# A decoder block on one Trainium2 core: chained VectorE work dealt out in single steps, rows reloaded a stage earlier, the turns' order changed

## What is computed

```
x = x + attn(layernorm(x), Wq, bq, Wk, bk, Wv, bv, Wo, bo)        # 16 heads of 128
x = x + xattn(layernorm(x), ctx, ctx, gamma)                     # 8 heads of 64 channels, over channels
x = x + ffn(layernorm(x), ternary(w1), ternary(w3), ternary(w2))  # hidden 1365, silu gate
```

## Time and profile before

| | us |
|---|---|
| median of 3 runs (1170.23 to 1171.52) | 1171.01 |
| the profiled execution | 1170.35 |
| its span, first to last instruction | 1168.6 |
| PE busy | 1118.9 |
| DVE busy | 743.5 |
| ACT busy | 551.6 |
| POOL busy | 461.0 |

### The profile page before, as it was taken

One profiled execution on the slowest core, in us unless ns is written; L12 is line 12 of the kernel. 1 busy time (PEld: TensorE's weight loads), 2 busy tenths in 40 slices (PEclk: granted clock), 3 DMA queues, 4 the chain that ended last, 5 costly groups with the idle time before them and its releaser, 6 DMA issues.

```text
span 1168.6 us, 15784 instructions
## 1 busy us (share of the span) xinstructions
PE 1118.9 (96%) x5792; PEld 938.8 (80%) x5792; DVE 743.5 (64%) x1389; ACT 551.6 (47%) x1145; POOL 461.0 (39%) x400
## 2 busy tenths in 40 slices
PE   4999999989999999999999999989999999999997
PEld 4888888868888788888888888768878887887776
DVE  7555547887757677765423325878767876787431
ACT  2455673324242366577514223267628753774230
POOL 1322327331432265664334030157517642764030
PEclk9999999999999999999999999999999999999999
DMA  7466654434433634312521022271113111310000
GB/s 234 132 181 180 197 162 138 163 112 146 143 115 121 204 91 120 98 37 98 225 72 55 18 97 82 94 201 47 46 56 107 46 47 64 99 46 11 27 1 36
DMA packets 53846, 121.13 MB, mean 104 GB/s; under 512 B 10009, under 2 KB 10009, under 8 KB 51722
## 3 DMA queue, kind: packets, MB, share of 16 engines
q1 hardware_dynamic: 53770, 120.13, 32.6%
HBM read 102.27 MB, written 17.84 MB: 103 GB/s over the span
## 4 chain that ended last, share of the span: by engine, by line
PE 83%; DVE 7%; ACT 4%; issue 2%; POOL 2%; DMA 1%; SPq 0%; POOLq 0%; DVEq 0%; ACTq 0%
PE bank L150 17%; PE bank L151 17%; PE bank L152 17%; PE bank L538 6%; PE bank L539 6%; PE bank L501 4%; PE bank L552 4%; PE bank L553 4%; PE bank L523 2%; PE bank L524 2%; PE bank L511 2%; PE bank L512 2%; POOL wal L1917 1%; DMA kd<-in_ctx 1%; ACT wah L1378 1%
## 5 line engine op out<-in xcount | busy, mean ns | idle before, releaser
L538 PE MATMUL bank<-x3h,w 128*128 128x512 f32 (+1 forms) x352 | 141.8, 403 | 2.4 <-DVE x3l L795 1.7
L1356 ACT ACTIVATE yh<-bank 128x512 fp32r<-128x512 f32 x64 | 38.1, 600 | 214.2 <-PE bank L152 214.1
L539 PE MATMUL bank<-x3l,w 128*128 128x512 f32 (+1 forms) x352 | 138.9, 394 | 0.0
L875 POOL TENSOR_SCALAR pe_x<-pe_x,xri,gam 128x512 f32<-128x512 f32 x96 | 75.6, 788 | 79.7 <-DVE xri L726 75.6
L150 PE MATMUL bank<-yh,rh 128*128 128x512 f32 x256 | 101.1, 395 | 6.0 <-DVE xacc L1779 6.0
L150 PE MATMUL bank<-wah,gh 128*128 128x512 f32 x256 | 103.9, 406 | 2.6 <-POOL wal L1917 1.3
L1917 POOL TENSOR_TENSOR wal<-raw_a,wah 128x512 fp32r<-128x512 f32 x44 | 59.7, 1382 | 117.2 <-ACT wah L1378 117.2
L722 DVE TENSOR_REDUCE xmx<-bank 128x1 f32<-128x512 f32 x128 | 87.5, 683 | 24.1 <-PE bank L512 23.3
L1922 POOL TENSOR_TENSOR wbl<-raw_b,wbh 128x512 fp32r<-128x512 f32 x64 | 88.6, 1408 | 36.0 <-ACT wbh L1398 35.8
L1615 DVE TENSOR_TENSOR yl<-bank,yh 128x512 fp32r<-128x512 f32 x64 | 44.0, 690 | 90.8 <-ACT yh L1356 90.6
L150 PE MATMUL bank<-wah,ph 128*128 128x512 f32 x256 | 100.4, 392 | 0.3 <-POOL wal L1917 0.3
(11 more groups left out here) (171 smaller groups left out, 3026.5 us busy)
## 6 DMA issues: line engine op xcount, KB each, us to landing
raw_a<-in_wk SPq DMA_DIRECT2D x8, 1024.0 KB, 5.3
raw_b<-in_wq SPq DMA_DIRECT2D x8, 1024.0 KB, 5.3
raw_a<-in_wo SPq DMA_DIRECT2D x8, 1024.0 KB, 5.1
raw_b<-in_wvt SPq DMA_DIRECT2D x8, 1024.0 KB, 4.9
ternary_scratch<-wraw SPq DMA_DIRECT2D x24, 341.2 KB, 2.9
x1d<-x_scratch SPq DMA_DIRECT2D x48, 128.0 KB, 3.1
kd<-in_ctx SPq DMA_DIRECT2D x48, 128.0 KB, 3.1
w<-ternary_scratch SPq DMA_DIRECT2D x2, 2730.0 KB, 10.8
```

What stands on the lines that cost most here:

```text
L538: pe.matmul(u_bank[w][0:m, :], lhs, x3h[:, c, :], start=c == 0, stop=False)
L539: mm = pe.matmul(u_bank[w][0:m, :], lhs, x3l[:, c, :], start=False, stop=c == CK - 1)
L875: pool.tensor_scalar(m.pe_x[:, q, :], m.pe_x[:, q, :], xri[:, q:q + 1], gam[:], ALU.mult, ALU.mult).then_inc(s["xpn"], 1)
```

## The change

- **Linked chains.** `newton_rsqrt` becomes `newton_step(k)`, one step a call. `bst`, `mvar`, `rstd`, `ntmp` and `nvar` get a place for each of two sequences. Four `bn_aggr` now share one link, and so do two `bn_stats`. In pass 0 (`dve_next_rows`) both sequences' moments come first, then their Newton steps together (128x8 elements) in two slots of six and seven steps, then the eight row tiles. `dve_x1` of sequence 1 goes one step (of `X1_STEPS` = 15) per early step 1 to 15; those of sequences 2 and 3 one step per step 1 to 30 of turn 1.
- **Rows of sequence 0.** They are loaded into a buffer of their own (`x2back`) in group j = 1 of pass 1; their moments, Newton steps and normalisation (`dve_back`) lie behind the `yl` splits of groups 1, 2 and 3. The rows to keep are loaded by a DMA (`sp_x2_kept`) and no longer copied, and the 1 MB load of sequence 1's x2 is issued before the last `out` tiles, ahead of the 2.7 MB load of w2, where it came behind it.
- **Turns.** `pe_vt` goes to the end of its step, behind the `pe_up` piece, for heads 0 and 4 one step later (`values_step`: steps 1, 8, 17, 24); `dve_vt` and `act_vt` move with it. The first `pe_up` piece of turns 2, 3 and last is made in two halves of 256 columns, each waiting for its own two `x3l` tiles. `pe_down` waits for each chunk's `gtl` by itself; tile 0 is split 5 and 6 chunks around a `pe_pt`, tile 1 3 and 8 around a `pe_ret`. The kept rows of turns 2, 3 and last are copied by POOL (`pool_keep`) instead of ACT.
- On SP the store of sequence 1's statistics goes behind group 3's loads, that of sequence 2 behind head 6.

```diff
@@ dve, linked chains
-    for _ in range(3):
+def newton_step(dve, link, y, tmp, v, k):
...
+        def dve_moments_in(dve, link, p, i, half):
+            dve.wait_ge(s[("xn_a", "xn_b")[half] + str(i)], 16 * (p + 1))
+            for j in (2 * half, 2 * half + 1):
+                ins = dve.bn_stats(bst[:, i, j, :], xnf[i][:, j, :])
+            link(ins)
+        def dve_aggregate(dve, link, i):
+            for j in range(TJ):
+                ins = dve.bn_aggr(mvar[:, i, j, :], bst[:, i, j, :])
+            link(ins)
...
+        def dve_next_rows(dve, link, part):
+            if 0 <= part < 4:
+                dve_moments_in(dve, link, 1, part // 2, part % 2)
+            elif part in (4, 5):
+                dve_aggregate(dve, link, part - 4)
+            elif part == 7:
+                for k in range(0, RSTD_STEPS // 2):
+                    dve_rstd(dve, link, slice(0, PB), k)
+            elif part == 8:
+                for k in range(RSTD_STEPS // 2, RSTD_STEPS):
+                    dve_rstd(dve, link, slice(0, PB), k)
+            elif 9 <= part < 9 + PB * TJ:
+                dve_normalise(dve, link, (part - 9) // TJ, (part - 9) % TJ)
...
-        def dve_early_values(dve, n):
+        def dve_early_values(dve, link, n):
             h, q = divmod(n, 4)
+            if 0 <= n - 1 < X1_STEPS:
+                dve_x1(dve, link, PASSES - 2, 1, n - 1)
...
             def attention_rest(n):
-                if n in (6, 10):
-                    dve_x1(dve, link, PASSES - 1, 1, n == 10)
+                i, k = divmod(n - 1, X1_STEPS)
+                if 0 <= i < PB:
+                    dve_x1(dve, link, PASSES - 1, i, k)
@@ rows of sequence 0
+        x2back = put("x2back", 112 * KB, [P, TJ, C])
...
         def sp_x2_back(sp):
-            sp.wait_ge(s["a_ready"], A["Y", PASSES - 1, GROUPS - 1, 0, CK - 1] + 1)
-            sp.dma_start(main.x2[:], x1_dram[0].rearrange("(t p) c -> p t c", p=P)).then_inc(s["x2_back"], 16)
+            sp.wait_ge(s["ptl"], GROUPS * (PASSES - 1) + 2)
+            sp.dma_start(x2back[:], x1_dram[0].rearrange("(t p) c -> p t c", p=P)).then_inc(s["x2_back"], 16)
...
                     dve_between(dve, link, p, j, c)
-                    if last and not further and c + 1 < CK:
-                        dve_moments_back(dve, c)
+                    if j and not further:
+                        dve_back(dve, link, CK * (j - 1) + c)
@@ stage_b_sp
-            sp_x2_back(sp)
...
             sp_head(sp, main, 1, 0)
             sp_head(sp, main, 1, 1)
+            sp.dma_start(main.x2[:], x1_dram[1].rearrange("(t p) c -> p t c", p=P)).then_inc(s["x2_in"], 16)
+            sp_x2_kept(sp)
             sp_x1_data(sp, p, 0)
-            sp_x1_stat(sp, p, 0)
             sp_x1_data(sp, p, 1)
             sp_head(sp, main, 1, 2)
             sp_w2(sp)
-            sp.wait_ge(s["x2_kept"], TJ)
-            sp.dma_start(main.x2[:], x1_dram[1].rearrange("(t p) c -> p t c", p=P)).then_inc(s["x2_in"], 16)
@@ turns
+        def values_step(h):
+            return 4 * h + (h % 4 == 0)
...
+            for cols in (slice(0, T // 2), slice(T // 2, T)) if piece == 0 and f else (slice(0, T),):
+                if piece == 0:
+                    pe.wait_ge(s["t_free"], t_x3(f, cols.stop // P))
...
-        def pe_down(pe, f, t):
-            pe.wait_ge(s["gl2"], 1 + f * HC + HC)
+        def pe_down(pe, f, t, chunks=range(HC)):
...
+                if t == 0:
+                    pe.wait_ge(s["gl2"], 1 + f * HC + i + 1)
...
-                        if q == 0 and h % 2 == 0:
-                            pe_vt(pe, main, b, h)
...
+                    if b is not None and h % 2 == 0 and values_step(h) == 4 * h + q:
+                        pe_vt(pe, main, b, h)
...
+                pe_down(pe, f, 0, range(0, HC // 2))
...
+                pe_down(pe, f, 0, range(HC // 2, HC))
...
+                pe_down(pe, f, 1, range(0, 3))
...
+        def pool_keep(pool, f, t):
+            pool.wait_ge(s["x3n"], (f + 1) * TJ)
+            pool.wait_ge(s["y_out"], 1 + f * (16 * TJ))
+            pool.tensor_copy(x2res[:, t, :], x2[:, t, :]).then_inc(s["x2_kept"], 1)
```

More of the change, by code:

```diff
@@ L892, in pool_turn @@
                 if f is not None:
+                    if f and n < TJ:
+                        pool_keep(pool, f, n)
                     for piece in pieces(n - GATE_LAG):
@@ L1889, in _ @@
             link = make_link(dve, "link", chain)
-            for part in range(LN_PARTS):
-                dve_normalise(dve, link, 0, 0, part)
+            dve_rows(dve, link, 0, 0)
             for j in range(TJ):
```

203 lines of the change are left out of this document (107 added, 96 removed).

## The result

The changed kernel takes **1157.24 us** (median of four runs, 1156.49 to 1157.44); the kernel before took 1170.62 on the same chip. The ratio is 0.9885, with a 95% interval of 0.9868 to 0.9902. The profiled execution took 1157.29, its span is 1155.5. The gain is 13 us; 20.7 were forecast.

A forecast was written before the change was run, and what follows sets the result against it. The prediction took TensorE (PE) to bound the kernel, busy 1118.9 us of 1168.6. Its terms summed to 20.7 us less than the profiled 1170.35, so 1149.65, with the median forecast at 1150; range 1144 to 1158.

The forecast's parts named there:

- rival 1: VectorE becomes the bound in turn 1, with small steps of 0.55 us filling its free time; 7.5 more, 1157 us; 18%.
- Start (-0.6): Before PE's first matmul: fewer links among `bn_aggr` and `bn_stats` bring DVE's first rows earlier, 0.6 us gained.
- Pass 0 (-5.1): Pass 0: without the late chain, PE's 4.02 us wait and the half clock go, 0.8 lost again; 5.1 us gained.
- Early steps (-0.4): Early steps of pass 1: a wait goes with the `dve_x1` lump (-1.4), fifteen single steps cost +1.0; 0.4 us gained.
- End of pass 1 (-1.9): End of pass 1: two PE waits of 0.8 us behind chains go, the moved chain costs 0; 1.9 us gained.
- Turn 1 (-1.1): Turn 1: step 10's lump goes (-2.8), `kd` lands earlier (-1.5), single steps cost +2.5, the start +0.7; 1.1 us gained.
- Values in mid-turn (-1.5): Middle of each turn: three waits of 0.6 us for `vts` go (-2.3), `dve_ret` costs +0.25 each; 1.5 us gained.
- Ends of turns (-5.1): Ends of turns 1 to 3: `pe_down` matmuls cover waits of 0.96 and 0.47 us; 1.7 gained each, 5.1 in all.
- Starts of turns 2 and 3 (+0.6): Starts of turns 2 and 3: no gain from the moves, `pool_keep` makes the first `pe_pt` late; +0.3 us each.
- Last turn (-0.9 and -4.7): Last turn: half the first piece precedes the last `x3l` (-0.9); `pe_down` needn't await all `gtl`, no half clock (-4.7 us).
- "Turn 1 about 87 us": Sign for turn 1: first score tile to last `pe_up` takes about 87 us instead of 90.1.
- Rival 3: Turn 1 and early steps: each small non-aggregating step waits for a whole POOL operation; 13 us slower, 1184; 3%.

The follow-up runs named there:

- six and six steps: Changed kernel with the twelve Newton steps of sequence 0's rows six and six behind the second and third `yl` of group 2, not four, four, four; 1156.58 us.
- faster version: Changed kernel with values at old place in turn 1, at new place with `dve_q` first in turns 2 and 3, Newton steps six and six; 1144.95 us.

## Why the prediction was right, and where it was not

Direction and range were right; 1157.2 is 7 us above the forecast time. It is the very number of rival 1, and rival 1 was wrong: its sign was a mean small step over 0.6 us in turn 1. The 38 small chain instructions there take 9.0 us in all, 0.24 each, which is also under the 0.4 forecast.

That the time stayed in the range is in part luck. With the values at their old place the turns take 4.7, 0.2 and 0.2 us less than before, where the forecast without the values' terms had 1.8 less in turn 1 and 0.3 more in each of the others. The move itself added 4.6, 2.1 and 2.3, where its terms come to +0.2, -0.5 and -0.5. So the move was forecast wrong by nearly 10 us, the rest of the turns made good some 4, and the range had been drawn wide for rivals that did not happen.

- *Start (-0.6).* Right by the first matmul, which shared links bring 0.56 us earlier in the mean of the executions. In the table it doesn't show, since the clock rose to full at 18.4 us in the one execution and at 19.8 in the other.
- *Pass 0 (-5.1).* Right: -5.1. The rounding instructions are still blocked (1.64 and 2.00 us at 236 and 238), and the bank still comes in time, all but 0.29. The cause was only half seen: with one link for the `bn_aggr` the lump costs 1.6, not 5, so most of this gain could have come from the links alone.
- *Early steps (-0.4).* -0.7; not tested alone.
- *End of pass 1 (-1.9).* Both waits went. The step that failed is "with POOL's splits later in the group: 0". The fourth `yl` is where POOL's splits of the next load begin; four Newton steps met them, 1.7 us of PE. The row to ask was the earlier trace rows itself. The run with six and six steps gives 2.0 back.
- *Turn 1 (-1.1).* The gains were undersized. `kd` is worth 2.2 and not 1.5 (x2's load behind w2's), and the single steps cost some 0.7, not 2.5: 20 of the 30 begin when POOL is idle. What the lump of step 10 cost by itself, forecast at 2.8, is not shown; two whole lumps cost 5.5 in the faster version, a stretch at half clock with them. The parts are measured in other kernels and do not add up exactly. Without the move of the values the turn would have taken 84.9; that it took 89.5 is the next point. There were waits over 1 us too, which the forecast's signs ruled out: 1.02 for `x3l` and 1.15 for the exponential.
- *Values in mid-turn (-1.5).* **The step that failed.** For step 17 it was right: there the wait for `vts` went. It asked what stands behind `dve_vt` at step 17 and did not ask at steps 8 and 24, where it is `dve_q`. There `dve_q` began 0.04 us behind POOL's `kl` and took 1.53 us in place of 0.53, and stood behind a `dve_vt` that waits. The move cost 9.0 us. With `dve_q` first 6.8 us of it come back; 3.3 are left in turn 1. PE's waits there are 4.5 us in that run and 1.9 with the values at their old place; three linked steps that fall beside POOL may be a part of it, but that was not tested by itself; in turns 2 and 3 the new place with `dve_q` first is even 0.6 us better than the old one.
- *Ends of turns (-5.1).* Right: -5.3, and the run with `pe_down` whole brings it back.
- *Starts of turns 2 and 3 (+0.6).* Right in sum: a gain of 1.1 at tile 1 is lost by tile 4, +0.1 each where +0.3 was forecast, with a wait of 1.35 there where 0.5 to 1 was named. `pool_keep` took 0.61 each, below both of its bounds (0.79 and 1.26).
- *Last turn (-0.9 and -4.7).* -1.1 and -4.7; the clock's part is shown by the window of the run with `pe_down` whole.
- *"Turn 1 about 87 us"* was a slip of the text: by its own terms 90.1 less 1.6 is 88.5. It took 89.9.

Rival 3 had the right mechanism at the wrong instruction. It asked it of the small steps, and these mostly come when POOL is idle, as the forecast said. The Trainium skill, "SBUF — State Buffer", section "SBUF: two separate sides", has the rule that fits: of a VectorE instruction in a two-port mode or with two inputs in SBUF, and a GpSimd one, whichever starts first holds the shared pair of ports for its whole length, and the other waits. The trace agrees: `dve_q`, at 0.53 us alone, took 1.53 when it began 0.04 after a `kl` of 1.29. That it runs in such a mode no run here shows by itself.

## What to carry to other kernels

For each instruction that is moved on VectorE, look at all its places, at the SBUF-only instruction that now stands behind it, and at what releases POOL's next long one: if one event upstream of both releases them, they can meet every time, as they did in six places of six here. A chain of tiny linked instructions belongs where POOL is idle; ask that of the new place with the same rows that condemned the old one. And when times move by 1 to 2 us without a reason, read stretches between the same matmuls, and the granted clock in each.
